# Turning the gated product on VectorE in 32x32 blocks, and projecting it with small matmuls

## Chip, cores, metric

One NeuronCore of a Trainium2 chip runs the whole program. The metric is the device time of one execution in microseconds, the median over the runs.

## What is computed

Two layers are applied one after another to x of shape (4, 32, 128, 128), batch, channels, height, width, in fp32. Each normalizes every channel of every image over its pixels, passes that through the block below and adds the result to x.

```python
def _forward(x, W_in, W_dw, fft_weight, W_out):      # DIM 32, HID 85, P 8
    xm = jnp.einsum('bchw,oc->bohw', x, W_in)
    x_spatial, x_freq, x_gate = jnp.split(xm, 3, axis=1)
    out_spatial = conv3x3_depthwise(x_spatial, W_dw)
    xp = x_freq.reshape(B, HID, h, P, w, P).transpose(0, 1, 2, 4, 3, 5)
    xi = jnp.fft.irfft2(jnp.fft.rfft2(xp) * fft_weight, s=(P, P))
    out_freq = xi.transpose(0, 1, 2, 4, 3, 5).reshape(B, HID, H, W)
    x_fused = gelu(x_gate) * (out_spatial + out_freq)
    return jnp.einsum('bchw,oc->bohw', x_fused, W_out)

x = x + block(groupnorm(x))     # twice, with its own weights each time
```

## The kernel before

**Tiles.** The image width is cut into four quarters (Q), which lie side by side on the partitions with 32 channels each. A strip is 8 columns wide in every quarter and 128 rows high. A strip has 8 tiles (TPS) of 16 x 8 pixels, 128 pixels, in each of the four quarters at once. There are 4 strips per image, 4 images, 2 layers: 32 strips, 256 tiles. A group is four tiles (GROUP, OUT), and a group of spectra has the number h.

**The loop.** Every engine runs its own copy of one loop over steps i, in order, and they meet at semaphores. `need(engine, semaphore, value)` is a wait. In step i TensorE works on tile i, and beside it on tiles a few steps ahead and behind:

- the convolution, 28 matmuls with the pixels of the tile as weights (128 x 128) and 85 columns streaming (L543), into ps_s, in four parts of seven, one for each quarter;
- four transposes of the product of tile i-2 (L594): pixels on the partitions go in, the 85 hidden channels on the partitions come out, in PSUM bank ps_ft. ScalarE copies them to ft (L765);
- in every fourth step (i % 4 == 2) the projection of four finished tiles (L616): four fp32 matmuls, one for each quarter, of 85 rows, 32 output columns and 512 pixels, into ps_o. VectorE scales that by osc and adds it to x (L1133);
- the gate, four matmuls (L549), in two pairs. ScalarE takes gelu of it into g (L770);
- the transposing matmuls of two tiles further ahead (`turn`, L511) in odd steps, and their transform (`transform`, L523, L524) in even ones;
- z, the frequency part of the projection for tile i+2 (L639), four matmuls from xs into ps_z, late in the step;
- two matmuls that turn the frequency part of tile i back to pixels and close ps_s (L654, L656).

z goes on to VectorE, which multiplies it by weff (y32, L1120); ScalarE makes the fp16 high part yh of it (L777), GpSimd the low part yl (L844). VectorE multiplies ps_s with gelu (L1097), the product.

**The spectra.** Four tiles' spectra leave PSUM together: the high part by ScalarE (L738), the low part by VectorE (L1045), into xf. Then they are brought from there into xs by twelve DMAs for each group h, three (k) for each quarter (q). GpSimd issues them (L425), those of quarter q in the step

```python
def loads_at(h, q):
    return {2: (3, 4, 4, 5), 3: (6, 7, 7, 8)}[h][q] if h < 4 else GROUP * h - 7 + q
```

and in its program they stand ahead of yl of the same step. z of tile 4h, in step 4h-2, waits for all twelve (`spectra_loaded`).

**The stacks.** The pixels of the convolution stand in `stack`, shifted copies of the strip in fp16, made from `parts` (ScalarE L707 high, VectorE L1029 low). There are two stacks. 28 DMAs fill one: 16 pairs (L305) and 12 thirds (L311). SyncE issues 24 of them and ScalarE four thirds, in the steps that THIRDS_BY_ACT names. The first copy of a strip waits until the strip before last is finished, and the convolution of a strip waits for all 28.

**Order on the other engines.** ScalarE in step i: the high part of the spectrum (every fourth), the copy of ps_ft, gelu of tile i, the copy of xt (odd steps), yh of tile i+2, the parts of the strip, DMAs. VectorE: product of tile i-1, the low part of the spectrum, the part of the strip or its normalization (odd steps), y32 of tile i+2, the sum of results (every fourth).

## Time and profile before

| | |
|---|---|
| median of 3 runs | 773.0 us |
| the runs | 770.43 to 773.76 us |
| the profiled execution's own time | 775.2 us |
| its span | 773.4 us |
| TensorE matmul, busy | 723.6 us (94%) |
| VectorE, busy | 545.1 us (70%) |
| ScalarE, busy | 572.5 us (74%) |
| GpSimd, busy | 624.1 us (81%) |
| granted TensorE clock, mean | 0.985 of full speed |
| DMA | 140.61 MB, 182 GB/s |

The profile is of one execution. An engine's busy time counts neither its waits nor the register and semaphore instructions. Matmuls are pipelined, so their durations overlap: one convolution matmul is shown with 203 ns, while one starts about every 41 ns. For TensorE the chain of waits is therefore the better measure: it gives each instruction only the time by which it moves the end. "Step" in this text is one pass of the loop, "period" the time from one projection to the next, four steps.

### The profile page before, as it was taken

Reading aid. Unit: us, or ns where it says so; the run is one execution under the profiler, and the core shown is the slowest. Engines: PE = TensorE matmul, PEld = TensorE weight load, DVE = VectorE, ACT = ScalarE, POOL = GpSimd, SP = SyncE. Lnnn points to the kernel's source line nnn. Section 1 sums busy time; section 2 is a strip of 40 time slices with the busy share of each in tenths; the row PEclk is TensorE's granted clock in tenths of the full one; section 3 lists DMA queues with packets and bytes.
Section 4 is the critical chain, followed back from the end, with each engine's and each line's share of the span. In section 5 each row is a group of like instructions: output and inputs, shape, how many; then the busy total and the mean of one; then the engine's idle time right before and its main releaser. Section 6 shows DMA issues by size and latency. Waiting matters only on the chain.

```text
span 773.4 us, 32267 instructions
## 1 busy us (share of the span) xinstructions
PE 723.6 (94%) x12324; PEld 620.0 (80%) x12324; DVE 545.1 (70%) x957; ACT 572.5 (74%) x1087; POOL 624.1 (81%) x1071
## 2 busy tenths in 40 slices
PE   2589989999999999999999999999999999999997
PEld 1477778877888878888788888889888988898875
DVE  7578867878877876777777687666666676667543
ACT  1676667777787778878887778787778777877754
POOL 1977777888888898888888987988788888988871
PEclk9689999999999999999999999999999999999999
DMA  8676888787767765677766766877767777787741
GB/s 299 162 182 174 195 181 211 170 190 174 180 177 191 182 160 152 163 167 182 189 171 165 166 183 176 216 190 199 190 176 192 194 199 204 194 209 191 191 129 56
DMA packets 96259, 140.61 MB, mean 182 GB/s; under 512 B 32498, under 2 KB 34746, under 8 KB 95978
## 3 DMA queue, kind: packets, MB, share of 16 engines
q1 hardware_dynamic: 64390, 103.30, 51.6%
q0 software_dynamic: 25376, 26.75, 14.1%
q10 hardware_dynamic: 6340, 8.49, 4.3%
q8 instruction: 99, 1.62, 1.0%
q14 instruction: 54, 0.44, 0.2%
HBM read 10.81 MB, written 8.54 MB: 25 GB/s over the span
## 4 chain that ended last, share of the span: by engine, by line
PE 72%; DVE 7%; issue 6%; POOL 6%; DMA 5%; ACT 2%; SPq 1%; ACTq 0%; POOLq 0%; DVEq 0%
PE ps_s L543 29%; PE ps_ft L594 12%; PE ps_o L616 7%; PE ps_g L549 5%; DMA xs<-xf 4%; PE ps_z L639 4%; PE ps_s L656 4%; PE ps_s L654 4%; PE ps_xt L511 3%; POOL xs L425 2%; PE ps_x L523 2%; PE ps_x L524 2%; POOL yl L844 1%; DVE y L1120 1%; POOL stack L305 1%
## 5 line engine op out<-in xcount | busy, mean ns | idle before, releaser
L543 PE MATMUL ps_s<-cw,stack 128*128 128x85 f16 (+1 forms) x7168 | 407.3, 203 | 1.8 <-DMA stack<-parts 1.6
L425 POOL DMA_DIRECT2D xs<-xf x757 | 385.2, 513 | 15.7 <-PE ps_z L639 12.5
L543 PEld LDWEIGHTS ps_s<-cw,stack 128*128 128x128 f16 (+1 forms) x7168 | 352.8, 99 | 27.4 <-issue 1.9
L844 POOL TENSOR_TENSOR yl<-y,yh 128x340 f16<-128x340 f32 x256 | 219.0, 856 | 105.2 <-ACT yh L777 103.1
L1120 DVE TENSOR_TENSOR y<-ps_z,weff 128x340 f32<-128x340 f32 x256 | 129.6, 506 | 136.8 <-PE ps_z L639 129.9
L777 ACT ACTIVATE yh<-y 128x340 f16<-128x340 f32 x256 | 124.6, 487 | 135.2 <-DVE y L1120 118.1
L1029 DVE TENSOR_TENSOR parts<-xn,parts 128x1024 f16<-128x1024 f32 (+2 forms) x99 | 126.9, 1284 | 63.8 <-ACT parts L707 63.5
L594 PE MATMUL ps_ft<-squares_sb,g 128*85 128x128 f32 x1024 | 163.4, 282 | 0.8 <-ACT turned_results L765 0.8
L765 ACT ACTIVATE turned_results<-ps_ft 85x512 f32<-85x512 f32 x256 | 149.3, 583 | 16.7 <-issue 10.0
L770 ACT ACTIVATE g<-ps_g,gsc 128x340 f32<-128x340 f32 x256 | 137.2, 536 | 18.7 <-PE ps_g L549 18.2
L1097 DVE TENSOR_TENSOR g<-ps_s,g 128x340 f32<-128x340 f32 x256 | 128.2, 501 | 11.0 <-PE ps_s L656 8.1
L549 PEld LDWEIGHTS ps_g<-pw,stack 128*128 128x128 f16 x1024 | 82.6, 98 | 55.2 <-issue 52.8
L549 PE MATMUL ps_g<-pw,stack 128*128 128x85 f16 x1024 | 125.0, 205 | 0.0
L594 PEld LDWEIGHTS ps_ft<-squares_sb,g 128*85 128x85 f32 x1024 | 115.3, 155 | 2.1 <-DVE g L1097 1.0
L707 ACT ACTIVATE parts<-xn 128x1024 f16<-128x1024 f32 (+2 forms) x99 | 100.3, 1017 | 14.4 <-DVE xn L1013 12.4
L639 PE MATMUL ps_z<-pw,xs 96*128 96x85 f16 x1024 | 81.5, 203 | 12.4 <-DMA xs<-xf 12.0
L654 PE MATMUL ps_s<-yh,waves 128*128 128x340 f16 x256 | 79.7, 311 | 0.0
L727 ACT ACTIVATE xt<-ps_xt 128x512 f16<-128x512 f32 x127 | 74.7, 588 | 6.7 <-PE ps_xt L511 4.2
L656 PE MATMUL ps_s<-yl,waves 128*128 128x340 f16 x256 | 79.0, 309 | 0.6 <-POOL yl L844 0.6
L616 PE MATMUL ps_o<-turned_results,wo 85*32 85x512 f32 x512 | 68.2, 605 | 1.3 <-ACT turned_results L765 0.7
L639 PEld LDWEIGHTS ps_z<-pw,xs 96*128 96x128 f16 x1024 | 54.9, 98 | 14.2 <-DMA xs<-xf 7.1
L523 PE MATMUL ps_x<-waves,xt 128*128 128x128 f16 x254 | 42.9, 222 | 13.7 <-DVE xf L1045 10.4
(108 smaller groups left out, 548.0 us busy)
## 6 DMA issues: line engine op xcount, KB each, us to landing
stack<-parts SPq DMA_DIRECT2D x496, 130.0 KB, 3.6
xs<-xf POOLq DMA_DIRECT2D x757, 32.0 KB, 2.8
out_y<-yo SPq DMA_DIRECT2D x16, 512.0 KB, 3.1
stack<-parts SPq DMA_DIRECT2D x93, 64.5 KB, 2.9
stack<-parts SPq DMA_DIRECT2D x93, 64.0 KB, 2.8
x<-in_x SPq DMA_DIRECT2D x16, 256.0 KB, 6.0
stack<-parts ACTq DMA_DIRECT2D x62, 65.0 KB, 3.8
stack<-parts SPq DMA_DIRECT2D x62, 65.0 KB, 2.8
```

The costliest lines, as they stand in the source:

```text
L425: eng.dma_start(xs[C * k:C * k + C, h % HELD, q, :], xf[C * q:C * q + C, h % 2, SPECTRA[k], :]).then_inc(loaded, 16)
L543: mm(ps_s[i % 2][:, HID * q:HID * (q + 1)], pixels(kind, i, q, dy, rows), w[0:rows, m, :], start=(q == 0 and m == 0), stop=False)
L549: t = mm(ps_g[:, HID * q:HID * (q + 1)], pixels(A, i, q, 0), pw[layer(i)][:, 1, :], start=(q == 0), stop=(q == Q - 1))
L594: t = nc.tensor.transpose(ps_ft[0:HID, q * 128:(q + 1) * 128], g[:, k, HID * q:HID * (q + 1)], id32)
L639: z = mm(ps_z[:, HID * q:HID * (q + 1)], xs[:, (i + 2) // GROUP % HELD, q, col:col + 128], pw[layer(i + 2)][0:3 * C, 0, :], start=(q == 0) ...
L765: nc.scalar.activation(ft[:, (i - 2) % (2 * OUT), :, :].rearrange("p q n -> p (q n)"), ps_ft[0:HID, 0:Q * 128], ACT.Copy).then_inc(s_ft, 1)
L770: nc.scalar.activation(g[:, i % 2, :], ps_g[:, 0:GC], ACT.Gelu, scale=gsc[layer(i)][:, 0:1]).then_inc(s_gelu, 1)
L777: nc.scalar.activation(yh[:, i % 2, :], y32[:, i % 2, :], ACT.Copy).then_inc(s_yh, 1)
L844: nc.gpsimd.tensor_tensor(yl[:, k, :], y32[:, k, :], yh[:, k, :], ALU.subtract).then_inc(s_yl, 1)
L1029: v.tensor_tensor(part[:, LO, rows], xn[:, rows, 1 + dx:1 + dx + TW], part[:, HI, rows], ALU.subtract).then_inc(s_xl, 1)
L1097: v.tensor_tensor(g[:, k, :], ps_s[k][:, 0:GC], g[:, k, :], ALU.mult).then_inc(s_f, 1)
L1120: v.tensor_tensor(y32[:, k, :].rearrange("p (q o) -> p q o", q=Q), ps_z[:, 0:GC].rearrange("p (q o) -> p q o", q=Q), weff[layer(i + 2)][:, ...
```

## The change

- The product goes to a new tile f with 96 columns per quarter (85 and zeros). VectorE transposes it from there into ft itself, in blocks of 32 x 32: within each block pixels and channels change places, the blocks stay where they are. The transposes of TensorE, the bank ps_ft and ScalarE's copy are gone.
- In ft the 32 channels of a block now lie on the 32 partitions on which their pixels were. So the projection runs over 32 rows at a time: for each of four row parts (two halves, two turns n), three channel blocks are accumulated, for four quarters. The halves write to two banks (ps_os). The second turn waits for the end of the first (s_o_half).
- The scale osc is multiplied into wo once per layer, so VectorE's sum of results is two additions, one for each bank.
- z stands behind the first part of the convolution in TensorE's step, not late in it. On VectorE the low part of the spectrum comes first, then the product, y32, the transpose, the part of the strip.
- yh and yl have three buffers (YS), y32 keeps two.
- Two of the twelve DMAs of a group's spectra (k = 0 and 1 of q = 0) are issued by ScalarE. ScalarE now issues two thirds of a strip, so SyncE issues 26 copies.

The diff, cut to its core:

```diff
+BLOCK = 32
+BLOCKS = -(-HID // BLOCK)
+YS = 3
...
-THIRDS_BY_ACT = {1: THIRDS[0:1], 2: THIRDS[1:2], 3: THIRDS[2:3], 4: THIRDS[3:4]}
+THIRDS_BY_ACT = {0: THIRDS[0:1], 4: THIRDS[1:2]}
+
+SPECTRA_BY_ACT = [(0, 0), (1, 0)]
...
+        wo = [sb(f"wo{i}", [128, BLOCKS, C]) for i in range(LAYERS)]
...
-        yh = sb("yh", [128, 2, GC], F16)
-        yl = sb("yl", [128, 2, GC], F16)
+
+        yh = sb("yh", [128, YS, GC], F16)
+        yl = sb("yl", [128, YS, GC], F16)
...
-        ft = turned_results[0:HID, :].rearrange("p (t q n) -> p t q n", q=Q, n=128)
+
+        f = sb("f", [128, 2, Q, BLOCKS * BLOCK])
+        ft = turned_results[:, :].rearrange("p (t q b n) -> p t q b n", q=Q, b=BLOCKS, n=BLOCK)
...
-        ps_xt, ps_x, ps_g, ps_z, ps_ft, ps_o = (bank(n) for n in ("ps_xt", "ps_x", "ps_g", "ps_z", "ps_ft", "ps_o"))
+        ps_xt, ps_x, ps_g, ps_z = (bank(n) for n in ("ps_xt", "ps_x", "ps_g", "ps_z"))
+
+        ps_os = [bank("ps_o0"), bank("ps_o1")]
+        ps_o = ps_os[0]
...
-                    pe.wait_ge(s_xs[h % HELD], 16 * 3 * Q * ((h - 2) // HELD + 1))
+                    pe.wait_ge(s_xs[h % HELD], 16 * (3 * Q - len(SPECTRA_BY_ACT)) * ((h - 2) // HELD + 1))
+                    pe.wait_ge(s_xs_act[h % HELD], 16 * len(SPECTRA_BY_ACT) * ((h - 2) // HELD + 1))
...
@@ -586,14 +602,18 @@
                     need(pe, s_f, i - 1)
                     conv_begins(i)
                     conv(i, 0)
-                if live(i, -2):
-                    k = i % 2
-                    need(pe, s_f, i - 1)
-                    need(pe, s_ft, i - 2)
+                if live(i, 2):
+                    if (i + 2) % LT == 0:
+                        pe.wait_ge(s_projection, PROJECTIONS * (layer(i + 2) + 1))
+                        pe.wait_ge(s_weff, layer(i + 2) + 1)
+                    if (i + 2) % GROUP == 0:
+                        spectra_loaded((i + 2) // GROUP)
+                    need(pe, s_y, i + 2)
+                    col = 128 * ((i + 2) % GROUP)
                     for q in range(Q):
-                        t = nc.tensor.transpose(ps_ft[0:HID, q * 128:(q + 1) * 128],
-                                                g[:, k, HID * q:HID * (q + 1)], id32)
-                    t.then_inc(s_ftp, 1)
+                        z = mm(ps_z[:, HID * q:HID * (q + 1)], xs[:, (i + 2) // GROUP % HELD, q, col:col + 128],
+                               pw[layer(i + 2)][0:3 * C, 0, :], start=(q == 0), stop=(q == Q - 1))
+                    z.then_inc(s_z, 1)
...
-                    for q in range(Q):
-                        o = mm(ps_o[C * q:C * q + C, :], wo[layer(tile)][:, :], ft[:, k:k + OUT, q, :],
-                               start=True, stop=True)
-                    o.then_inc(s_o, 1)
+                    if tile % LT == 0:
+                        pe.wait_ge(s_wo_scaled, layer(tile) + 1)
+
+                    for n in range(2):
+                        if n == 1:
+                            pe.wait_ge(s_o_half, tile // OUT + 1)
+                        for block in range(BLOCKS):
+                            for half in range(2):
+                                rows = slice(BLOCK * (2 * half + n), BLOCK * (2 * half + n + 1))
+                                out = ps_os[half][:, 0:OUT * 2 * BLOCK].rearrange("p (t n x) -> p t n x", n=2, x=BLOCK)
+                                for q in range(Q):
+                                    o = mm(out[C * q:C * q + C, :, n, :], wo[layer(tile)][rows, block, :],
+                                           ft[rows, k:k + OUT, q, block, :],
+                                           start=(block == 0), stop=(block == BLOCKS - 1))
+                        o.then_inc((s_o_half, s_o)[n], 1)
...
-                if live(i, 2):
-                    if (i + 2) % LT == 0:
-                        pe.wait_ge(s_projection, PROJECTIONS * (layer(i + 2) + 1))
-                        pe.wait_ge(s_weff, layer(i + 2) + 1)
-                    if (i + 2) % GROUP == 0:
-                        spectra_loaded((i + 2) // GROUP)
-                    need(pe, s_y, i + 2)
-                    col = 128 * ((i + 2) % GROUP)
-                    for q in range(Q):
-                        z = mm(ps_z[:, HID * q:HID * (q + 1)], xs[:, (i + 2) // GROUP % HELD, q, col:col + 128],
-                               pw[layer(i + 2)][0:3 * C, 0, :], start=(q == 0), stop=(q == Q - 1))
-                    z.then_inc(s_z, 1)
...
-                    s, k = ps_s[i % 2], i % 2
+                    s, k = ps_s[i % 2], i % YS
...
-                if live(i, -2):
-                    need(act, s_ftp, i - 1)
-                    need(act, s_o, (i - 2 - 2 * OUT) // OUT + 1)
-                    nc.scalar.activation(ft[:, (i - 2) % (2 * OUT), :, :].rearrange("p q n -> p (q n)"), ps_ft[0:HID, 0:Q * 128],
-                                         ACT.Copy).then_inc(s_ft, 1)
                 if live(i, 0):
                     need(act, s_gate, i + 1)
-                    need(act, s_ftp, i - 1)
+                    need(act, s_f, i - 1)
                     nc.scalar.activation(g[:, i % 2, :], ps_g[:, 0:GC], ACT.Gelu,
                                          scale=gsc[layer(i)][:, 0:1]).then_inc(s_gelu, 1)
...
                 if live(i, 2):
                     need(act, s_y, i + 3)
-                    need(act, s_s, i + 1)
-                    nc.scalar.activation(yh[:, i % 2, :], y32[:, i % 2, :], ACT.Copy).then_inc(s_yh, 1)
+                    need(act, s_s, i + 3 - YS)
+                    nc.scalar.activation(yh[:, (i + 2) % YS, :], y32[:, i % 2, :], ACT.Copy).then_inc(s_yh, 1)
...
+                for h in range(2, GROUPS_OF_TILES):
+                    for n, (k, q) in enumerate(SPECTRA_BY_ACT):
+                        if loads_at(h, 0) + n == i:
+                            load_row(act, h, q, k, s_xs_act[h % HELD])
...
                 for h in range((i + 4) // GROUP, (i + 7) // GROUP + 1):
                     for q in range(Q):
                         if 2 <= h < GROUPS_OF_TILES and loads_at(h, q) == i:
-                            load_spectrum(pool, h, q, s_xs[h % HELD])
+                            for k in range(3):
+                                if (k, q) not in SPECTRA_BY_ACT:
+                                    load_row(pool, h, q, k, s_xs[h % HELD])
                 if live(i, 2):
-                    k = i % 2
-                    need(pool, s_s, i + 1)
+                    k, k3 = i % 2, (i + 2) % YS
+                    need(pool, s_s, i + 3 - YS)
                     need(pool, s_yh, i + 3)
-                    nc.gpsimd.tensor_tensor(yl[:, k, :], y32[:, k, :], yh[:, k, :], ALU.subtract).then_inc(s_yl, 1)
+                    nc.gpsimd.tensor_tensor(yl[:, k3, :], y32[:, k, :], yh[:, k3, :], ALU.subtract).then_inc(s_yl, 1)
...
+                link(v.tensor_scalar(osc[l][:, :], p2[:, l, 0:1], p2[:, l, 1:2], 1.0 / SS, ALU.mult, ALU.mult))
+                dve.wait_ge(s_wo, 16 * LAYERS)
+                v.tensor_scalar(wo[l][:, :, :].rearrange("p b c -> p (b c)"), wo[l][:, :, :].rearrange("p b c -> p (b c)"),
+                                osc[l][:, 0:1], None, ALU.mult).then_inc(s_wo_scaled, 1)
...
             for i in steps():
+                if i in leaving:
+                    lo_of_spectrum(leaving[i])
                 if live(i, -1):
                     k = (i - 1) % 2
                     need(dve, s_s, i)
                     need(dve, s_gelu, i)
-                    v.tensor_tensor(g[:, k, :], ps_s[k][:, 0:GC], g[:, k, :], ALU.mult).then_inc(s_f, 1)
-                if i in leaving:
-                    lo_of_spectrum(leaving[i])
-                def split_beside():
...
-                if i == (STRIPS - 2) * TPS:
-                    norm(STRIPS)
+                    v.tensor_tensor(f[:, k, :, 0:HID], ps_s[k][:, 0:GC].rearrange("p (q o) -> p q o", q=Q),
+                                    g[:, k, :].rearrange("p (q o) -> p q o", q=Q), ALU.mult).then_inc(s_f, 1)
...
                                     ALU.mult).then_inc(s_y, 1)
+                if live(i, -1):
+                    dve.wait_ge(s_f, i)
+                    need(dve, s_o, (i - 1 - 2 * OUT) // OUT + 1)
+                    v.transpose(ft[:, (i - 1) % (2 * OUT), :, :, :].rearrange("p q b n -> p (q b n)"),
+                                f[:, (i - 1) % 2, :, :].rearrange("p q h -> p (q h)")).then_inc(s_ft, 1)
+                def split_beside():
...
+                if i == (STRIPS - 2) * TPS:
+                    norm(STRIPS)
...
-                    v.scalar_tensor_tensor(xv if l + 1 < LAYERS else staging,
-                                           ps_o[:, :].rearrange("p (r w) -> p r w", w=TW),
-                                           osc[l][:, 0:1], xv, ALU.mult, ALU.add).then_inc(s_res, 1)
+                    for half in range(2):
+                        old, new = (r.rearrange("p (t s r) w -> p t s r w", t=OUT, s=2)[:, :, half, :, :]
+                                    for r in (xv, xv if l + 1 < LAYERS else staging))
+                        o = v.tensor_tensor(new, ps_os[half][:, 0:OUT * 2 * BLOCK].rearrange(
+                            "p (t r w) -> p t r w", t=OUT, w=TW), old, ALU.add)
+                    o.then_inc(s_res, 1)
...
-        arrays[f"w_out{l}"] = np.ascontiguousarray(raw["W_out"].T)
+        w_out = np.zeros((BLOCKS * BLOCK, C), np.float32)
+        w_out[0:HID] = raw["W_out"].T
+        arrays[f"w_out{l}"] = np.ascontiguousarray(np.tile(w_out.reshape(BLOCKS, BLOCK, C).transpose(1, 0, 2), (128 // BLOCK, 1, 1)))
```

## Rows read from the trace of the kernel before

**Rows 1.** The page, busy time of each engine and share of the span.
```profile
PE 723.6 (94%) x12324; PEld 620.0 (80%) x12324; DVE 545.1 (70%) x957; ACT 572.5 (74%) x1087; POOL 624.1 (81%) x1071
```

**Rows 2.** Chain of waits, 500 to 525 us: start, time on the chain, what.
```profile
502.80 0.08 PE ps_g L549 x2
...
506.61 0.47 PE ps_ft L594 x4
...
507.16 0.28 PE ps_s L543 x7
507.45 0.23 PE ps_xt L511 x4
...
507.75 0.57 PE ps_s L543 x14
508.32 0.15 PE ps_z L639 x4
508.47 0.15 PE ps_s L654
...
509.52 0.99 PE ps_o L616 x8
510.52 0.19 PE ps_g L549 x2
...
511.64 0.15 PE ps_z L639 x4
...
520.62 0.99 PE ps_o L616 x8
```

**Rows 3.** Timeline of SyncE's DMA issues, 522 to 550 us: start, duration, what.
```profile
525.87 11.86 SPq L305 DMA_DIRECT2D stack<-parts  x16
537.77 5.19 SPq L311 DMA_DIRECT2D stack<-parts  x8
...
547.81 2.57 SPq L305 DMA_DIRECT2D stack<-parts  x4
```

**Rows 4.** Waits in 100 to 700 us: total, times, longest.
```profile
PE ps_x L523 <- DVE xf L1045: 7.2, 12, 0.8
...
PE ps_z L639 <- DMA xs<-xf: 4.0, 6, 1.9
```

**Rows 5.** One old projection: timeline of its matmuls and loads, and their durations.
```profile
509.45 0.16 PEld L616 LDWEIGHTS ps_o<-turned_results,wo 85*32 85x32 f32 x8 [0.15 <-issue]
509.45 1.06 PE L616 MATMUL ps_o<-turned_results,wo 85*32 85x512 f32 x8
...
L616 PEld LDWEIGHTS ps_o<-turned_results,wo x512: 106/108/109, 57.3 to 768.5; 85*32 85x32 f32 x171
L616 PE MATMUL ps_o<-turned_results,wo x512: 592/605/617, 57.3 to 768.9; 85*32 85x512 f32 x171
```

**Rows 6.** Timeline of GpSimd, 500 to 512 us, and its DMAs' landing, 400 to 700.
```profile
504.82 0.85 POOL L844 TENSOR_TENSOR yl<-y,yh 128x340 f16<-128x340 f32 x1
505.60 1.49 POOL L425 DMA_DIRECT2D xs<-xf  x3
...
DMA to landing us min/median/max: 1.7/2.8/4.5
```

**Rows 7.** Timeline of ScalarE, 500 to 508 us.
```profile
502.91 0.55 ACT L770 ACTIVATE g<-ps_g,gsc 128x340 f32<-128x340 f32 x1
503.36 0.59 ACT L727 ACTIVATE xt<-ps_xt 128x512 f16<-128x512 f32 x1
504.18 0.49 ACT L777 ACTIVATE yh<-y 128x340 f16<-128x340 f32 x1 [0.24 <-DVE y L1120]
```

**Rows 8.** VectorE: its groups, mean ns of one; its busy time in a stretch.
```profile
L1120 DVE TENSOR_TENSOR y<-ps_z,weff 128x340 f32<-128x340 f32 x256 | 129.6, 506 | 136.8 <-PE ps_z L639 129.9 <-POOL yl L844 5.5 <-issue 0.2
L1133 DVE SCALAR_TENSOR_TENSOR yo<-ps_o,osc,x 128x512 f32<-128x512 f32 x32 | 23.8, 742 | 4.3 <-PE ps_o L616 4.3
...
100.00:400.00 300.00, 228.17 (x392) 0.99 0.73 176
```

More of the change, by code:

```diff
@@ L150, in build @@
         weff = [sb(f"weff{i}", [128, HID]) for i in range(LAYERS)]
-        wo = [sb(f"wo{i}", [HID, C]) for i in range(LAYERS)]
-        gsc = [sb(f"gsc{i}", [128, 1]) for i in range(LAYERS)]
-        osc = [sb(f"osc{i}", [128, 1]) for i in range(LAYERS)]
+        wo = [sb(f"wo{i}", [128, BLOCKS, C]) for i in range(LAYERS)]
+        columns = sb("columns", [128, 2 * LAYERS + 3])
+        gsc = [columns[:, i:i + 1] for i in range(LAYERS)]
+        osc = [columns[:, LAYERS + i:LAYERS + i + 1] for i in range(LAYERS)]
+        ve, power, table = (columns[:, 2 * LAYERS + i:2 * LAYERS + i + 1] for i in range(3))
         st = [sb(f"st{i}", [128, 2 * STRIPS, 6]) for i in range(LAYERS)]
@@ L247, in build @@
         s_xs = [sem(f"s_xs{i}") for i in range(HELD)]
+        s_xs_act = [sem(f"s_xs_act{i}") for i in range(HELD)]
         s_z = sem("s_z")
@@ L255, in build @@
         s_f = sem("s_f")
-        s_ftp = sem("s_ftp")
         s_ft = sem("s_ft")
         s_o = sem("s_o")
+        s_o_half = sem("s_o_half")
         s_res = sem("s_res")
```

39 lines of the change are left out of this document (19 added, 20 removed).

## The prediction, on record before the changed kernel was seen

> **What bounds the kernel now.** I read the busy times first: TensorE is busy 94% of the span, GpSimd 81%, nobody else above 74% [rows 1]. The chain of waits then says what this busy time is worth. In the steady part it is TensorE alone, with hardly a gap, and the projection of one group of four tiles lies 11.10 us before the next (509.52 to 520.62). One step, the work of one tile, is the sum of short pieces: 0.28 for the first seven convolution matmuls, 0.47 for the four transposes, 0.08 and 0.08 for the gate, 0.28 and 0.57 for the rest of the convolution, 0.23 for the turn or the transform, 0.15 for z and 0.15 for each of the last two matmuls (one of the two is shown): 2.44 [rows 2]. The fourth step also has the projection: 0.99, and 0.11 more in the first gate pair behind it (0.19 against 0.08). 4 x 2.44 + 1.10 = 10.9; the rest is small waits. So a microsecond taken off TensorE's step is worth one microsecond, until another chain takes over. Two are close. SyncE issues the copies of a strip of eight tiles in 11.86 + 5.19 us, and the strip lasts 21.94 us (525.87 to 547.81) [rows 3]. And the copies of the spectrum (xs), which GpSimd issues, must have landed before z of every fourth tile; TensorE waits for them only 4.0 us in the 600 us looked at [rows 4].
>
> **What is removed.** The transposes: 256 x 0.47 = 120 us. The old projection: 64 x 1.10 = 70 us. Both are on the chain of TensorE, so 190 us go. ScalarE also loses the copy of the turned product, which frees it but is off the path.
>
> **The new projection.** Per group there are 2 turns (n) x 3 blocks x 2 halves x 4 quarters = 48 matmuls of 128 columns, in fp32, so 96 after the split in two passes that the old one shows (4 matmuls in the code, 8 in the trace) [rows 5]. No row shows a 32x32 piece of the array at work. The old matmuls used 85 rows by 32 columns of it, four pieces beside each other: eight matmuls of 512 columns in 0.99 us, so four ran at once and a pass cost 0.50 us, or 0.124 us for 128 columns. If the pieces of the two halves (other rows, other PSUM bank) also run at once, each piece has 3 x 2 passes per turn, 0.74 us, and the two turns take 1.49. Between the turns TensorE waits for its own last result (s_o_half): a matmul's record lasts 605 ns of which about 500 are its pass, so 0.1 for the tail and about as much for the signal and the new start, 0.2. Entering and leaving cost what the old one paid, 0.11, on both sides, and the eight pieces start one behind another: 0.36 in all. Together 2.05 us per group, 131 us in all. Bounds: from below 12 passes at the price of a transpose (0.47 / 4 = 0.118), 1.4, plus 0.1: 1.5. From above there are two. If the halves do not overlap, 24 passes x 0.124 + 0.56 = 3.5. If a small matmul with its weight load costs the spacing of the convolution's, 0.57 / 14 = 0.041, then 96 x 0.041 + 0.4 = 4.3. I take 2.05, since the eight weight loads of the old projection, 108 ns each, fit in 0.16 us together, some 7 ns apart [rows 5]: small pieces are started far faster than one in 41 ns.
>
> The Trainium skill ("TensorE: Matmul & The Clock Gate", Back-to-back issue gap) gives every matmul a floor of about 25 ns from start to start, however small; the loads 7 ns apart and the four 605 ns matmuls that ran side by side do not show such a floor between different pieces. By the page the 96 matmuls would take 2.4 us, and the new projection about 2.9; by the rows it is 2.05.
>
> **z moved to the front, and what it waits for.** This is where I expect the time to go back. z of tile 4h is computed in step 4h-2 and needs the spectra of group h, all twelve copies. The last three (q=3) are issued by GpSimd in its step 4h-4, behind yl of tile 4h-3. That yl needs yh, which ScalarE makes in its step 4h-5 behind gelu and behind the copy of xt. Count from the start of step 4h-5. Before, z of tile 4h was at the end of step 4h-2, three steps and then almost another later. In the trace the three copies start at 505.60 and take 1.49, so the last is issued at 506.6 and lands 2.8 us later, 509.4 (up to 4.5 later at worst) [rows 6]; z is at 511.64 [rows 2]. About 2 us to spare.
>
> After: the three light steps shrink from 2.44 to 1.97, and z stands only 0.28 into its step: z wants its data at 3 x 1.97 + 0.28 = 6.19 us. The chain: the gate ends at 0.28 + 0.15 + 0.08 + 0.28 + 0.23 + 0.08 = 1.10, gelu starts 0.03 later (502.88 to 502.91), the xt copy 0.45 behind it, yh 0.50 behind that (they come every 0.45 to 0.5 when back to back) [rows 2, 7]: 2.08. yh takes 0.49 and yl starts 0.15 later (504.18 + 0.49 = 504.67, 504.82) [rows 6, 7]: 2.72. The copies start 0.78 behind yl (505.60 - 504.82): 3.50; the last of three is issued 1.0 later: 4.50. With the median landing of 2.8 it is 7.3, but z waits for the latest of twelve copies, so I take 3.2 and 7.7. TensorE stands still for 1.5 us in every group: 60 groups x 1.5 = 90 us. Bounds: below, a landing at the minimum of 1.7 gives 6.2, no stall; above, 4.5 gives 9.0, a stall of 2.8. That y comes earlier on VectorE, the third buffer of yh and yl and the two spectra copies given to ScalarE (q=0, the first of the group) do not shorten this chain, for it hangs on gelu ahead of yh in ScalarE's order and on the last copies, not the first. Queued behind z in TensorE's order are the new projection and the whole rest of the step, so nothing hides the stall. It takes in the 4.0 us that TensorE already waits for xs, and the 7.2 us that it waits for xf [rows 4], since the low part of the spectrum is now VectorE's first work in its step.
>
> **VectorE.** It is busy 228 of 300 us in the first layer [rows 8], 8.4 per group. The transpose of 384 elements is new. Nearest is the operation on 340 elements with 506 ns; by length 0.57; from below half of that, if a single source without PSUM runs faster, from above twice that, 1.1, if it needs two passes. I take 0.55. The sum of results is two operations of 256 in place of one of 512 with 742 ns; from 506 and 742 a 256 is about 0.39, so +0.04. 8.4 + 4 x 0.55 + 0.04 = 10.7 per group, under TensorE's 11.7 (below): it costs nothing as long as the period stays above 10.7. Its wait for s_o in front of the sum ends with TensorE's step 1.5 us from its end, and the sum and statistics behind it take about that. ScalarE loses 0.58 per tile and gains two short issues per group. GpSimd loses two issues of 0.5. Zeroing f, scaling wo and the larger wo load are some tenths of a microsecond at the start.
>
> **SyncE.** Two more copies per strip, 11.86/16 or 5.19/8 = 0.65 to 0.74 each: 17.05 + 1.4 = 18.4, and about 2.8 until the last has landed, 21.2 us per strip. It cannot start before the strip before last is done, so this is a floor of the strip, 10.6 per group: hidden behind 11.7, decisive if TensorE gets faster.
>
> **Sum**, against the profiled run's own 775.2: -120 - 70 + 131 + 90 - 4 - 7 = 795. The median is 2.2 below the profiled run, so 793 us. The period per group goes from 11.1 to about 8.1 + 2.05 + 1.5 = 11.7.
>
> **Rivals.**
> *The spectra are in time* (other side: faster). If the copies land in 1.7 to 2.2 us or yh gets through earlier, the stall goes. TensorE alone would need 8.1 + 2.05 = 10.2 per group, 20.4 per strip; then SyncE's 21.2 sets the strip. Against 21.94 before that is 0.8 to 1.0 less per strip, 31 strips, and VectorE's 10.7 in the first layer holds it there: 773 - 29 = 744. By the sum, 703 + 60 x stall, the time is back at 773 at a stall of 1.16; below that this case decides. For it: 1.7 is a landing that occurs. Against: 2.8 is the median and the last of twelve counts.
> *Halves one behind another*: 3.5 in place of 2.05, 64 x 1.5 = 93 more: 886. For it: no row shows two row parts at once. Against: nothing in the columns did serialise.
> *Issue floor* as on the page named above, worked out with a piece started every 25 ns: 2.9 per group, +52: 845.
> *VectorE the bound*: transpose at 1.1, 8.4 + 4.4 = 12.8 per group in the first half, 1.1 x 30 over 11.7: 826.
> *No change in time*: the same sum with a stall of 1.1 to 1.2 gives 769 to 775, gain and stall cancel.
>
> **How the numbers follow.** The stall case 0.50 (its own range 768 to 822, from the stall between 1.1 and 2.0), spectra in time 0.28, halves in turn 0.09, issue floor 0.04, VectorE 0.04, no change 0.05. The range 738 to 845 leaves out the halves in turn, part of the issue floor and a third of the fast case. About 0.5% (4 us) is what a measurement of this kernel can tell from none. Faster 0.31 (the fast case and a tail of the stall case), same 0.09, slower 0.60.
>
> **What would show it.** In the changed profile: no transposes on TensorE; the projection's group on the chain of waits near 2.05 per four tiles (3.5 if the halves take turns); TensorE's z waiting for DMA of xs by 60 to 120 us in all; group period 11.7; the transpose on VectorE near 0.55; SyncE idle before a strip's first copy by a few us. The prediction is wrong if z waits less than 40 us in all for xs, or the projection is off by more than half a microsecond.

## The result, and the profile after

The changed kernel takes 887.9 us (median of 4 runs, 884.16 to 895.42) against 772.7 us for the kernel before (4 runs): ratio 1.151, 95% interval 1.143 to 1.159. 793 was forecast, with 738 to 845 as the range. The profiled execution took 889.56 us, its span is 887.8 us. Five profiles below (z late, four thirds, both late with eight thirds, last quarter by ScalarE, large projection) are of executions 0.8 to 1.3% above the medians of their kernels, so their busy times, waits and clocks are a little off, and the clocks in the table near the end are medians over the undisturbed executions.

The page of the changed kernel: busy time of each engine, and the TensorE clock that was granted, in tenths, over 40 slices of the span.
```profile
PE 735.4 (83%) x16932; PEld 647.4 (73%) x16932; DVE 659.1 (74%) x1280; ACT 435.1 (49%) x831; POOL 562.5 (63%) x947
...
PEclk9688888988879989998998988989878889998898
```
TensorE was meant to have 723.6 - 120 - 70 + 131 = 665 us of work; it is busy for 735. And it is idle for 887.8 - 735.4 = 152 us, where it was idle for 773.4 - 723.6 = 50 [rows 1]. The clock row is no longer a row of nines: its mean is 0.881, against 0.985 before.

The same page: groups by line, idle time before them and what ended it.
```profile
L1126 DVE TENSOR_TENSOR f<-ps_s,g 128x340 f32<-128x340 f32 x256 | 128.4, 501 | 79.3 <-PE ps_s L675 78.3
L1132 DVE TENSOR_TENSOR y<-ps_z,weff 128x340 f32<-128x340 f32 x256 | 129.1, 504 | 69.2 <-PE ps_z L614 68.2
L614 PE MATMUL ps_z<-pw,xs 96*128 96x85 f16 x1024 | 86.7, 212 | 112.3 <-DMA xs<-xf 111.1
...
L1139 DVE STREAM_TRANSPOSE turned_results<-f 128x384 f32<-128x384 f32 x256 | 144.8, 565 | 0.1
L646 PE MATMUL ps_o<-turned_results,wo 32*32 32x128 f32 x6144 | 134.4, 300 | 6.5 <-DVE turned_results L1139 1.2
```
z now waits 111 us for the copies of the spectra (4.0 in [rows 4]), in 61 waits: 1.8 us each. VectorE waits for TensorE and not the other way round; the transpose, which had no row before [rows 8], takes 565 ns.

The chain of waits, 503 to 530 us, with one group at each clock (compare [rows 2]).
```profile
502.99 0.46 PE ps_s L558 x7
503.44 0.15 PE ps_z L614 x4
503.68 0.28 PE ps_s L558 x7
503.96 0.23 PE ps_xt L526 x4
504.50 0.25 issue
504.74 0.59 ACT xt L746
505.33 0.39 ACT yh L792
505.86 0.50 POOL yl L867
506.36 0.28 issue
506.63 0.22 POOL xs L441
506.86 0.28 issue
507.14 0.49 POOL xs L441
507.63 3.81 DMA xs<-xf
511.49 0.33 PE ps_z L614 x4
511.81 1.06 PE ps_o L646 x48
512.92 1.53 PE ps_o L646 x48
...
515.36 1.00 PE ps_s L558 x14
...
522.70 3.91 DMA xs<-xf
526.65 0.33 PE ps_z L614 x4
526.98 0.90 PE ps_o L646 x48
527.92 0.93 PE ps_o L646 x48
```
Three things can be read here. First, the loop of the forecast stands in it piece by piece: copy of xt, yh, yl, the three issues of GpSimd, the landing, z. From the start of the step (502.99) yl starts after 2.87 us, and the last of the three copies is issued after 4.64 (at 507.63, where the landing begins in the chain); the forecast said 2.72 and 4.50. From there to the landing it is 3.8 and 3.9 us in the two groups shown, where I had taken 3.2. TensorE itself stands still for less than that, since it still has work when the copy is issued: 1.78 us ahead of 511.49 and 2.24 us ahead of 526.65. Second, the new projection: 0.90 + 0.93 us at full clock, with the step between the turns 1.9. Third, the half that ran from 512.92 took 1.53 us, and the fourteen convolution matmuls behind it 1.00 where they take 0.57 [rows 2]: TensorE was granted 1.2 GHz and not 2.4. This follows directly on the stall of 1.78 us and the first half of the small matmuls. The clock of the second group did not fall, although its stall was longer.

### The profile page after: what moved, and what is told of

Same layout as the page of the kernel before. It is cut to its first block, busy times and chain, and to the rows that moved or that the text cites. A ratio compares the mean times of both kernels' runs of the same rounds, so it can differ in the third digit from the quotient of the medians.

```text
span 887.8 us, 41236 instructions
## 1 busy us (share of the span) xinstructions
PE 735.4 (83%) x16932; PEld 647.4 (73%) x16932; DVE 659.1 (74%) x1280; ACT 435.1 (49%) x831; POOL 562.5 (63%) x947
## 4 chain that ended last, share of the span: by engine, by line
PE 41%; DMA 22%; issue 12%; POOL 10%; ACT 6%; DVE 3%; SPq 2%; ACTq 1%; POOLq 0%; DVEq 0%
DMA xs<-xf 22%; PE ps_o L646 15%; PE ps_s L558 13%; POOL xs L441 6%; POOL yl L867 4%; PE ps_g L564 4%; PE ps_z L614 4%; ACT xt L746 3%; ACT yh L792 2%; PE ps_s L673 1%; PE ps_s L675 1%; PE ps_xt L526 1%; PE ps_x L538 1%; ACTq L441 1%; PE ps_x L539 1%
## 5 line engine op out<-in xcount | busy, mean ns | idle before, releaser
L558 PE MATMUL ps_s<-cw,stack 128*128 128x85 f16 (+1 forms) x7168 | 450.5, 216 | 3.2 <-DVE f L1126 1.9
L558 PEld LDWEIGHTS ps_s<-cw,stack 128*128 128x128 f16 (+1 forms) x7168 | 391.7, 107 | 36.6 <-DVE f L1126 5.3
L441 POOL DMA_DIRECT2D xs<-xf x633 | 320.5, 510 | 13.7 <-PE ps_z L614 5.4
L785 ACT ACTIVATE g<-ps_g,columns 128x340 f32<-128x340 f32 x256 | 138.3, 540 | 376.2 <-PE ps_g L564 375.9
L1126 DVE TENSOR_TENSOR f<-ps_s,g 128x340 f32<-128x340 f32 x256 | 128.4, 501 | 79.3 <-PE ps_s L675 78.3
L1132 DVE TENSOR_TENSOR y<-ps_z,weff 128x340 f32<-128x340 f32 x256 | 129.1, 504 | 69.2 <-PE ps_z L614 68.2
L614 PE MATMUL ps_z<-pw,xs 96*128 96x85 f16 x1024 | 86.7, 212 | 112.3 <-DMA xs<-xf 111.1
L1139 DVE STREAM_TRANSPOSE turned_results<-f 128x384 f32<-128x384 f32 x256 | 144.8, 565 | 0.1
L646 PE MATMUL ps_o<-turned_results,wo 32*32 32x128 f32 x6144 | 134.4, 300 | 6.5 <-DVE turned_results L1139 1.2
L564 PE MATMUL ps_g<-pw,stack 128*128 128x85 f16 x1024 | 135.0, 218 | 0.0
L646 PEld LDWEIGHTS ps_o<-turned_results,wo 32*32 32x32 f32 x6144 | 94.1, 112 | 30.2 <-PE ps_o L646 24.1
L526 PE MATMUL ps_xt<-id,parts 128*128 128x128 f16 x508 | 53.2, 231 | 4.3 <-DVE parts L1055 4.3
```

Source lines behind the costliest of these rows:

```text
L441: eng.dma_start(xs[C * k:C * k + C, h % HELD, q, :], xf[C * q:C * q + C, h % 2, SPECTRA[k], :]).then_inc(loaded, 16)
L558: mm(ps_s[i % 2][:, HID * q:HID * (q + 1)], pixels(kind, i, q, dy, rows), w[0:rows, m, :], start=(q == 0 and m == 0), stop=False)
L564: t = mm(ps_g[:, HID * q:HID * (q + 1)], pixels(A, i, q, 0), pw[layer(i)][:, 1, :], start=(q == 0), stop=(q == Q - 1))
L614: z = mm(ps_z[:, HID * q:HID * (q + 1)], xs[:, (i + 2) // GROUP % HELD, q, col:col + 128], pw[layer(i + 2)][0:3 * C, 0, :], start=(q == 0) ...
L646: o = mm(out[C * q:C * q + C, :, n, :], wo[layer(tile)][rows, block, :], ft[rows, k:k + OUT, q, block, :], start=(block == 0), stop=(block ...
L785: nc.scalar.activation(g[:, i % 2, :], ps_g[:, 0:GC], ACT.Gelu, scale=gsc[layer(i)][:, 0:1]).then_inc(s_gelu, 1)
```

## The experiments

Each ratio is against the kernel before, timed beside it in the same session (772.5 to 774.1 us). A "theory" is one of the outcomes that the text put on record ahead of the run gives.

**z late, and z and y late.** The changed kernel with z back at the end of TensorE's step; then y32 also back behind the transpose on VectorE.
```diff
 conv(i, 0)
-z(i + 2)
 projection ...
+z(i + 2)     # behind the last two matmuls of the step
```


> The changed kernel with z back at the late place of TensorE's step, all else as changed. Theory A (the wait for the spectra is the loss, and the half clock comes from that wait): z wants its data about 1.6 us later, so its wait for xs falls from 111 us to under 20, the granted clock returns to over 0.97, and the time is 740 to 775; VectorE now waits for the late z with the transpose behind it, which may hold it at the upper end. Theory B (the small matmuls themselves lower the clock or cost more than they show): the clock stays under 0.92 and the time over 820.

> As the one before, and y32 also back behind the split of the strip in VectorE's step, so that the transpose does not stand behind the wait for z. Theory A: 740 to 760, VectorE waits for z only where it has nothing else, clock over 0.97. If the order on VectorE does not matter, the same as the one before within 4 us. Theory B: over 820.

Measured: 819.1 us (1.059, 1.055 to 1.063) and 794.5 us (1.028, 1.023 to 1.032). The waits of the first:
```profile
DVE y L1132 <- PE ps_z L658: 155.6, 129, 5.8
PEld ps_x L538 <- issue: 64.1, 56, 2.0
PE ps_x L538 <- DVE xf L1071: 57.9, 56, 1.9
```
z's wait for the copies is nearly gone (8.4 us), and the mean granted clock is back at 0.951. But y32 is first in VectorE's order and now waits for a z that comes last, and everything of VectorE queues behind it, the transform's result among it. With y late too, this wait falls to 68.6 us and the clock is 0.965. So with late copies the early places of z and y cost 93 us (888 to 795), clock included; and z late alone only trades a wait for the copies against one on VectorE. Both times are above the first theory's ranges (740 to 775 and 740 to 760): it had z's wait right and the clock nearly, and made too little of the waits of VectorE.

**The copies one step earlier**, z and y as in the changed kernel. This takes away what makes z late, not z's place.
```diff
-            return {...}[h][q] if h < 4 else GROUP * h - 7 + q
+            return {...}[h][q] if h < 4 else GROUP * h - 8 + q
```


> The changed kernel with all xs copies from the fourth group on issued one step earlier (4h-8+q in place of 4h-7+q), z still first. Theory A: the last copies no longer stand behind yl of tile 4h-3 and land at about 4.7 us after the start of step 4h-5, z wants them at 6.2: wait for xs under 20 us, clock over 0.97, time 735 to 755 with SyncE's copies of a strip as the next bound. Theory B: no better than 850.

Measured: 777.8 us (1.006, 1.003 to 1.009), 110 us less than the changed kernel, yet above the 735 to 755 of the first theory. TensorE is busy for 669.8 us, clock 0.961; z waits 10.4 us. The chain of this kernel, by engine, and SyncE's issues, 488 to 531 us:
```profile
SPq 44%; PE 30%; DVE 8%; issue 8%; DMA 6%; ACT 2%; POOL 1%; ACTq 1%; DVEq 0%; POOLq 0%
```
```profile
488.42 13.20 SPq L321 DMA_DIRECT2D stack<-parts  x16
501.66 8.36 SPq L327 DMA_DIRECT2D stack<-parts  x10
510.06 0.59 SPq L452 DMA_DIRECT2D out_y<-yo  x1
510.75 11.89 SPq L321 DMA_DIRECT2D stack<-parts  x16
522.68 8.16 SPq L327 DMA_DIRECT2D stack<-parts  x10
```
SyncE goes from one strip into the next with hardly a pause, 22.3 us (488.42 to 510.75) in the first one shown; the next begins 21.8 us later, at 532.55. The strip of before took 21.94 with room in it [rows 3]. 20.1 to 21.6 us of issues and the store leave little or nothing: with the spectra in time, the 26 copies are the bound, as the run with 24 copies below confirms. The rival expected 744 here, from 21.2 us per strip.

**The stall filled.** Sixteen extra matmuls of 256 columns ahead of the z that needs a new group; their result is written over by z.
```diff
+if i >= 6 and (i + 2) % GROUP == 0:
+    for _ in range(16):
+        mm(ps_z[:, 0:256], bas, waves, start=True, stop=True)
```


> The changed kernel with 16 extra matmuls of 256 columns (1.7 us at the full clock) ahead of z in every fourth step, in the time that TensorE waits for xs; they add work that nobody reads and change no result. Theory A: they stand in the wait, the granted clock rises from 0.88 to over 0.97, and since the wait itself stays the time falls by what the half clock costs, about 60 to 75 us: 812 to 830. If the half clock costs nothing beyond the wait: 885 or more. Theory B: no change of the clock, about 890 to 960.

Measured: 858.6 us (1.112, 1.107 to 1.116), 29 us less than the changed kernel although it does more. The group that was added, on the page:
```profile
L612 PE MATMUL ps_z<-waves 128*128 128x256 f16 x992 | 118.5, 272 | 0.0
```
The clock is 0.971 and z waits 33.1 us. The ledger prices the clock: 887.9 + 118.5 (added work) - 78 (111.1 - 33.1 of stall used up) = 928; measured 858.6; so 70 us came back with the clock. TensorE's busy time says somewhat more: without the added group it is 774.1 - 118.5 = 656 us, 80 less than in the changed kernel. The time is above the 812 to 830 of the first theory, which took the added matmuls to fit into the stall: they are 118 us long, and it shrank by 78.

**The kernel before with z first**, nothing else of the change.
```diff
 conv(i, 0)
+z(i + 2)
 transposes ...
-z(i + 2)     # late in the step
```


> The kernel before with one part of the change alone: z moved to behind the first part of the convolution in TensorE's step. Theory A (the early z meets late spectra, whatever the projection is): z wants its data at 3 x 2.44 + 0.28 = 7.6 us after the start of step 4h-5, the copies land at about 8.4, so TensorE waits about 0.8 per group, 30 to 70 us in all, and the clock falls in part: 800 to 840. Theory B (only the shorter step of the changed kernel makes the copies late): no wait, 765 to 778.

Measured: 870.7 us (1.125, 1.118 to 1.132). What its z waited for, from its waits:
```profile
PE ps_z L598 <- DMA xs<-xf: 57.7, 33, 7.6
PE ps_z L598 <- DVE y L1120: 41.5, 63, 1.2
```
The move of z alone, in the old kernel with its transposes and large projection, costs 97 us. Its z stands 99 us in all, as much as the changed kernel's but for a tenth, and still the granted clock stays at 0.967. 870.7 is above both theories (800 to 840, and 765 to 778): the first foresaw the late copies and left out the wait for y.

**Fewer copies for SyncE.** The version with early copies, with four (as before) and with eight thirds of a strip copied by ScalarE, so that SyncE issues 24 and 20; then the eight-thirds version with z and y late. The diff is that of the four thirds.
```diff
-THIRDS_BY_ACT = {0: THIRDS[0:1], 4: THIRDS[1:2]}
+THIRDS_BY_ACT = {1: THIRDS[0:1], 2: THIRDS[1:2], 3: THIRDS[2:3], 4: THIRDS[3:4]}
```


> The changed kernel with the xs copies one step earlier and four thirds of a strip on ScalarE again (SyncE 24 copies in place of 26). Theory A (SyncE's issues and their landing are the period of the strip now): two issues less are 1.4 us per strip, 31 strips, so 778 - 43 = 735, or up to 750 where VectorE or TensorE takes over. Rival (VectorE, 84% busy, is the bound and SyncE only follows): 770 to 778.

> As the one before, with eight of the twelve thirds on ScalarE (SyncE 20 copies). Theory A: SyncE is no longer a bound; TensorE's 10.2 and VectorE's 10.7 per group set it: 722 to 742, and not more than 15 below the one before. Rival: 770 to 778.

> As the one before, but with z late in TensorE's step and y32 late in VectorE's, the order of the kernel before. If the moved orders of the change are worth something once the copies are in time: slower than the one before by 10 to 30 (VectorE waits for the late z, its 84% has no room for it). If they are worth nothing: the same within 5.

Measured: 757.3 us (0.980, 0.975 to 0.985), 761.5 us (0.983, 0.979 to 0.987) and 785.0 us (1.010, 1.003 to 1.017). Two copies less for SyncE are worth 20 us; four more are worth nothing, since its share of the chain is then no more than VectorE's (12% each). The first theories' ranges (735 to 750, 722 to 742) were missed by 7 and 19 us, on the slow side. The chain by engine with 24 copies:
```profile
PE 43%; SPq 25%; DMA 11%; DVE 7%; issue 7%; POOL 3%; ACT 2%; ACTq 1%; DVEq 0%; POOLq 0%
```
And once the copies are in time, z first and y first are worth 785.0 - 761.5 = 24 us (the executions of the late version spread over 14 us): the order was right for a kernel whose copies land.

**The last quarter by ScalarE.** The changed kernel, where ScalarE issues two copies (k = 0 and 1) of q=3 and not of q=0. Its loop issues them in steps 4h-7 and 4h-6, where GpSimd had issued them in step 4h-4 behind the critical yl; the third copy of q=3 stays there, with GpSimd.
```diff
-SPECTRA_BY_ACT = [(0, 0), (1, 0)]
+SPECTRA_BY_ACT = [(0, 3), (1, 3)]
```


> The changed kernel with one thing else: the copies of the last quarter of a spectrum (fourth copy of both halves) go to ScalarE in place of those of the first quarter, so that GpSimd, which issues last, issues two and not three behind its yl. Theory A (the stall at z is the chain up to the last copy's issue and its landing): the last issue of GpSimd comes about 0.5 us earlier, so 62 groups give back about 30 us, and the half-clock time that goes with the stall some 10 to 20 us more: 835 to 850 us against 888, TensorE's wait of z for the copies 80 to 90 us in place of 111. Theory B (the landings themselves are the stall, whoever issues): no change within 0.5%. Theory C (ScalarE's issue stands ahead of its next pieces and delays them): slower than 888.

Measured: 797.9 us (1.028, 1.020 to 1.035), 90 us less than the changed kernel. Its GpSimd, 504 to 506 us, and z on its page:
```profile
504.47 0.85 POOL L867 TENSOR_TENSOR yl<-y,yh 128x340 f16<-128x340 f32 x1
505.25 0.51 POOL L441 DMA_DIRECT2D xs<-xf  x1
```
```profile
L614 PE MATMUL ps_z<-pw,xs 96*128 96x85 f16 x1024 | 84.7, 208 | 45.3 <-DMA xs<-xf 43.4
```
Behind the critical yl stands one issue and not three, so the last one goes out 1.0 us earlier and not 0.5 as I had written; with that slip the expectation of 835 to 850 was far too high. z waits 43 us and not 111: 68 us from 61 groups, 1.1 us each. TensorE's busy time falls by another 42 us (735.4 to 693.5; clock 0.928, and 0.947 in the other executions). This is the cleanest proof of the chain: one line with a constant, 10%. The run does not separate the earlier last issue from the two copies that went out some steps earlier. The change gave ScalarE the first quarter's copies, which nobody waits for.

**Two buffers, and the last quarter by ScalarE, in the best version** (757.3 us).
```diff
-YS = 3
+YS = 2
```


> The best version so far (copies one step earlier, four thirds on ScalarE, 757.3 us) with two buffers of yh and yl in place of three. Theory A (VectorE's turning waits for nothing of TensorE in this version; two buffers are enough): 755 to 761 us. Theory B (the third buffer lets VectorE run a step ahead through the strip's boundary, where TensorE waits for a strip): VectorE waits for the projection's matmuls, 765 to 785 us.

> The best version so far (757.3 us) with the copies of the last quarter on ScalarE in place of those of the first. Theory A (with the copies one step ahead the landing has slack everywhere, so who issues them is nothing): 755 to 760 us. Theory B (ScalarE's issues now stand ahead of its own piece of the chain): 762 to 775 us.

Measured: 772.2 us (0.998, 0.994 to 1.002) and 758.5 us (0.979, 0.974 to 0.985). The third buffer is worth 15 us there. The time is in the second theory's range, but the wait is not the one it named. With two, yh waits for the matmul that reads the buffer:
```profile
ACT yh L792 <- PE ps_s L675: 65.9, 98, 1.8
```
Who issues the last quarter is nothing once all copies go out a step earlier, as the first theory said.

**The projection moved away from z.** The changed kernel with the small matmuls at the end of the step.
```diff
 z(i + 2)
-projection
 gate, conv(i, 1) ... conv(i, 3)
+projection
```


> The changed kernel with one thing else: the small matmuls of the projection stand behind all of the step's convolution and not between its z and the rest, so the stall ahead of z and the 32-row matmuls are apart. The stall of z for the copies should stay near 110 us in all theories. Theory A (the granted clock falls because the stall and the small matmuls follow one another): mean granted clock 0.95 or more in place of 0.881, and 825 to 845 us against 888. Theory B (both have only to be there in a step, wherever): clock 0.87 to 0.90 and 880 to 895 us. Theory C (the small matmuls, later, hold up the next step's chain, which starts with the convolution's sums, or not at all): clock as in A and the wait of z shorter too, since the gate and the sums come some 2 us earlier in the step: 760 to 800 us.

Measured: 875.3 us (1.128, 1.120 to 1.136), clock 0.905, z waits 94.1 us. At the edge of the second theory and far from the other two: the stall and the small matmuls need not touch each other. Apart, they lower it less often, though: ahead of z there are 43 pauses of 0.5 us and more and 15 falls of the clock behind them, against 54 and 38 in the changed kernel.

**Large matmuls in place of the small ones; the small ones twice.** The first leaves the projection's result out: 16 matmuls of 128 x 256 in fp16 stand where the 96 small ones stood. The second is the best version with each half of the projection issued twice.
```diff
-for block ... for half ... for q ...: o = mm(out[32 rows], wo[rows, block], ft[rows, ...])
+for _ in range(8):
+    o = mm(ps_os[n][:, 0:256], bas, waves, start=True, stop=True)
```


> The changed kernel with the 96 small matmuls of a projection left out and 16 matmuls of 128 rows by 256 columns in fp16 in their place (119 ns each in the filled kernel, so 1.9 us in all, as the small ones took); the results added to the pixels are not the reference's. All waits, and with them the stall of z for the copies, stay: about 110 us by all theories. Theory A (the granted clock falls through small matmuls and stalls together): clock 0.95 or more, 800 to 840 us. Theory B (the stall of the late copies is enough to lower the clock): clock 0.87 to 0.90 and 875 to 890 us.

> The best version so far (757.3 us, granted clock 0.961, no stall of the copies to speak of) with each half of a projection's small matmuls issued twice; the result is the same sum. Theory A (small matmuls lower the clock only where TensorE also stalls): clock 0.95 or more; 64 times 1.9 us more on TensorE, 122 us, of which what is idle today (762 less 671, some 90 us) takes a part: 790 to 880 us. Theory B (the small matmuls alone lower the clock, in proportion to their time): clock below 0.93 and 850 to 930 us.

Measured: 838.5 us (1.081, 1.077 to 1.086), clock 0.933 (0.945 to 0.950 in the other executions), stall 101 us; and 951.4 us (1.226, 1.219 to 1.233), clock 0.885. For the first run that is the edge of the first theory (clock 0.95 or more, 800 to 840 us) and outside the second: with large matmuls in place of the small ones, nearly the same stall (101 against 111 us) costs 5% of the clock and not 12%. The page and the clock row of the second run:
```profile
PE 832.9 (87%) x23076; PEld 739.2 (78%) x23076; DVE 650.9 (68%) x1280; ACT 437.1 (46%) x831; POOL 550.9 (58%) x947
...
PEclk9578889998988997898899798988989997898898
```
z waits only 9.5 us for the copies there, TensorE is busy 87% of the time, and still the clock falls as far as in the changed kernel. That looks as if small matmuls needed no stall at all, but the trace says otherwise. The doubled matmuls brought pauses of their own. TensorE's waits in it, and its chain through one projection:
```profile
PE ps_o L647 <- issue: 46.0, 40, 2.6
PE ps_s L558 <- issue: 16.7, 14, 2.2
```
```profile
520.98 1.56 PE ps_o L647 x96
522.58 0.89 PE ps_o L647 x42
523.47 0.82 issue
524.28 1.07 PE ps_o L647 x53
...
525.97 1.00 PE ps_s L558 x14
```
In the middle of the small matmuls TensorE stands still for 0.8 us with no releaser that the profile shows, and the convolution behind it runs at 1.2 GHz (1.00 us for fourteen matmuls, 0.57 at 2.4). What the pauses are, no run shows. 40 of the 64 projections have a pause of 0.3 us or more inside, and the clock fell in or behind 29 of them. In the other 24 it fell seven times, once behind a stall of z and otherwise in the pauses of the step that follows. So the run does not show that small matmuls lower the clock without a pause, and the theory that it takes both still stands. The time is 951.4 - 757.3 = 194 us more; of the 190 between the profiled spans, 110 are the added matmuls (234.2 busy against 124.3), some 52 the same other instructions at the lower clock, and 29 more idle time.

**Parts of the change, or of its cure, in the kernel before.** SyncE with 26 copies; the copies of the spectra one step earlier; z first with the earlier copies.

> The kernel before with one thing else: two thirds and not four copied by ScalarE, so that SyncE issues 26 copies for a strip as in the changed kernel. Theory A (SyncE's copies take 21.2 us a strip, TensorE's own work in the kernel before some 22 us a strip, so they don't bind): 770 to 777 us. Theory B (the copies already bind at 26, and the changed kernel lost by them too): 780 us or more.

> The kernel before with the copies of the spectra one step earlier and nothing else. Theory A (TensorE's own work binds it, and it waits only 4.0 us for the copies): 768 to 774 us, so that the 2% of the best version come from the turning by VectorE. Theory B (the earlier copies are worth 2% in any kernel): 755 to 762 us.

> The kernel before with z first in TensorE's step (870.7 us) and the copies one step earlier. Theory A (the late copies were the loss of that order): 772 to 790 us; what stays is the wait of z for y of VectorE, 66 us there, part of which falls with the stall. Theory B (y, late on VectorE, is what binds it): 800 to 850 us.

Measured: 777.4 us (1.004, 1.002 to 1.007), 768.8 us (0.993, 0.991 to 0.995) and 829.9 us (1.071, 1.067 to 1.075). 26 copies cost 4 us there. The earlier copies give 5 us; the other 11 us of the best version (768.8 to 757.3) come with the turning by VectorE and the order that goes with it, which no run separates. The first time is at the edge of the first theory's range and the second within it; the third is in the range of the second theory. z first is not cured in the kernel before by the copies alone:
```profile
L598 PE MATMUL ps_z<-pw,xs 96*128 96x85 f16 x1024 | 81.9, 204 | 75.7 <-DVE y L1120 62.7
```
z now waits for y, which VectorE makes late in its step. This half of the order (y first on VectorE) the change had right.

**The clock over the runs.** In all 19 profiles together, from 60 us on and without the last 20, there are 220 stretches at 1.2 GHz. Each of them begins in or right behind a pause of TensorE of 0.5 us or more. The kernel before has one, behind its only long stall of z in that time; from its timeline and its chain, 108 to 117 us:
```profile
111.62 0.33 PE L639 MATMUL ps_z<-pw,xs 96*128 96x85 f16 x4 [1.95 <-DMA xs<-xf]
```
```profile
112.83 0.50 PE ps_s L543 x7
...
116.49 0.28 PE ps_s L543 x7
```
The table counts the pauses ahead of z by their length in the profiled execution of each kernel, in the same part of it, and in how many cases the clock fell in the pause or at most 4 us behind it. "Small" is small matmuls for each projection, z's wait that for the copies in us.

| kernel | small | z's wait | pauses of 0.5 to 1.5 us, falls | of 1.5 us and more, falls | granted clock, median | us |
|---|---|---|---|---|---|---|
| before | 0 | 4 | 2, 0 | 1, 1 | 0.987 | 772.7 |
| before, z first | 0 | 58, and 42 for y | 72, 0 | 15, 7 | 0.966 | 870.7 |
| changed, large projection | 0 | 101 | 17, 1 | 30, 23 | 0.950 | 838.5 |
| copies early | 96 | 10 | 0, 0 | 0, 0 | 0.957 | 777.8 |
| stall filled | 96 | 33 | 14, 3 | 5, 5 | 0.969 | 858.6 |
| last by ScalarE | 96 | 43 | 17, 8 | 8, 7 | 0.947 | 797.9 |
| projection later | 96 | 94 | 18, 1 | 25, 14 | 0.905 | 875.3 |
| changed | 96 | 111 | 22, 11 | 32, 27 | 0.884 | 887.9 |
| small twice | 192 | 10 | 3, 1 | 0, 0 | 0.893 | 951.4 |

Two things can be read in it. After long pauses the clock falls whatever stands behind: in 23 of 30 cases with the large projection, in 7 of 15 in the z-first kernel of before, in 27 of 32 with small matmuls. After short ones it falls often where small matmuls stand right behind z (11 of 22, and 8 of 17), less where extra matmuls fill the stall ahead of z (3 of 14), and hardly ever without small matmuls right behind (0 of 72, 1 of 17, 1 of 18). The kernel with early copies has no such pause ahead of z; six of its nine falls came with a pause ahead of the convolution, where it waits for the stack.

## Why the prediction was wrong

The direction and the mechanism of the stall were right, the amount was not: 95 us too little. The account on TensorE, by the profiled runs: busy 735 against 665, 70 us; idle 152 against 50 + 90 - 4 - 7 = 129, 23 us. The period of a group, forecast as 11.7 us, was 13.0 on average.

- **The failed step is the sum**, which counts "-120 - 70 + 131" at the full clock. It has no term for the granted clock. Its size by three ways: 735.4 - 669.8 = 66 us, against the same instructions with early copies (clock 0.961); 70 us by the ledger of the filled stall; and 80 us by TensorE's busy time in it. The work itself was counted well: the 656 us of the filled kernel, at a clock of 0.971, stand against 665. Together with the stall it also put the range's upper end below the result. The page of before, whose clock row is nines from the fourth slice on, hides it; the trace of before had it, in the one stall of 1.95 us with 3.4 us at half clock behind it, and a forecast of a stall of 1.5 us in every group could have made it a rival.
- **The stall, mis-sized.** "TensorE stands still for 1.5 us in every group: 60 groups x 1.5 = 90 us" measured 111 us, 1.8 us each. The chain up to the last issue was right within 0.15 us; the landing, taken as 3.2, was 3.8 to 3.9 in the two groups shown. The bound of 2.8 us held for the mean and not for every group: single waits reached 4.8 us between 115 and 800 us.
- **The new projection, right.** 2.05 forecast, about 1.9 at full clock. The halves do overlap, and *halves one behind another* is out. The 48 matmuls of one turn took 0.93 us, so one started every 19 ns. The Trainium skill ("TensorE: Matmul & The Clock Gate", Back-to-back issue gap) gives about 25 ns from start to start; between matmuls on different 32 x 32 pieces the trace is below it, and the *issue floor* is out.
- **VectorE, right.** 0.55 forecast, 0.565 measured; it waits for TensorE in the changed kernel (78.3 and 68.2 us), as foreseen. *VectorE the bound* is out.
- **SyncE's floor, right in kind and a little low.** 21.2 us per strip forecast, hidden in the changed kernel; it came out when the copies were in time: 22.3 and 21.8 us in the strips shown, 777.8 us in all. *The spectra in time* named this bound, but gave 744; the 20.1 to 21.6 us of issues alone stood where 18.4 had been counted.
- **Nothing hides the stall**, right: filled with 118 us of work the kernel still got faster.
- "The prediction is wrong if z waits less than 40 us": it waited 111, and the projection was off by 0.15. Both tests passed, and the time was still outside. They did not ask for the clock.

The z-first kernel of before (0.966) and the one with a large projection (0.950) have no small matmuls and stand still ahead of z for about as long (99 and 101 us). What differs is the length of the single pauses: 15 of 1.5 us and more against 30. What stays open is why a short pause is enough beside small matmuls, and what the pauses inside the doubled projection are. No run here shows either.

## What to carry to other kernels

When an operation is moved ahead in an engine's order, follow the data that it reads back to the last issue of its last transfer, and count that chain in the new, shorter steps: here 2 us of room turned into 1.8 us of stall for each group, and one constant (who issues the last copies) or one step of lead brought 90 to 110 us back. Before counting gains on TensorE, ask what its clock will be: here pauses of 1.5 us and more lowered it in most cases, shorter ones where small matmuls stood right behind, and a change that brings both pays on all its matmuls (66 to 80 us). When a cure works, look at who is next; here SyncE's copies took the path as soon as the stall was gone, which was worth 20 us more, and only with both removed was the change worth 2%.

## What was not expected of the hardware

- Matmuls on different 32 x 32 pieces start 19 ns apart on average (48 in 0.93 us), and those of two row halves run side by side.
- Every fall of the clock in these traces came with a pause of TensorE, even in the kernel with 192 small fp32 matmuls for each projection, where TensorE was busy 87% of the span and its mean granted clock was 0.885. Pauses of 0.5 to 1.5 us were followed by a fall in 11 of 22 cases with small matmuls right behind them, in 1 of 17 with large ones.
- A block of 192 small matmuls did not run through: TensorE paused inside 40 of 64 such blocks, 0.3 to 2.6 us, with nothing in the profile that it waited for.
- A copy of 32 KB took 3.8 to 3.9 us from its issue to its landing where it was the last of twelve issued (two groups), against a median of 2.4 on the page for all that GpSimd issued.
